# Decoder layer on one core: context loads behind the next x, expert weights split and a routed product moved ahead of the barrier

## The reference

```
x = x + attn(layernorm(x))          # own layernorm again, attention over the 256 features of a sequence, projection, + its input
x = x + xattn(layernorm(x), ctx)    # c, c2q, c*c2q, c*q2c concatenated, times W_l
x = x + moe(layernorm(x))           # 8 experts of 256 -> 128 -> 256, 4 chosen per token by grouped routing, and a shared one
```

## Time and profile before

| | us |
|---|---|
| median of 3 runs (lowest, highest) | 705.83 (705.38, 708.27) |
| profiled execution | 705.53 |
| its span | 703.7 |
| TensorE busy in it | 665.9 |
| mean granted clock of TensorE (1 is 2.4 GHz, 0.5 is 1.2 GHz) | 0.992 |
| VectorE, ScalarE, POOL busy | 474.3, 359.3, 249.8 |

### The profile page before, as it was taken

How to read it: one execution, slowest core, us unless ns; L and a number is a source line. 1 busy time by engine, 2 the same in 40 slices (tenths; PEclk the granted TensorE clock), 3 DMA queues, 4 the chain that set the end, 5 groups by cost and what they waited for, 6 DMA issues and landing times. The chain is left out here.

```text
span 703.7 us, 11790 instructions
## 1 busy us (share of the span) xinstructions
PE 665.9 (95%) x3880; PEld 563.4 (80%) x3880; DVE 474.3 (67%) x1237; ACT 359.3 (51%) x826; POOL 249.8 (35%) x321
## 2 busy tenths in 40 slices
PE   3999999899999999999989879999999999999997
PEld 2778878778788788787877767888888888888886
DVE  4488675676776776767778977666766666676433
ACT  3656674665667566756666536342333424234321
POOL 2136264064172462641734403232223222222231
PEclk9999999899999999999999999999999999999999
DMA  8616044043052150430541443321213232130300
GB/s 215 167 27 172 10 111 117 0 117 110 0 167 60 49 171 7 113 114 0 165 134 31 116 170 112 121 90 58 104 50 121 89 120 89 46 125 11 122 30 31
DMA packets 51775, 64.44 MB, mean 92 GB/s; under 512 B 3913, under 2 KB 49529, under 8 KB 50849
## 3 DMA queue, kind: packets, MB, share of 16 engines
q1 hardware_dynamic: 51744, 64.06, 30.0%
HBM read 56.60 MB, written 7.45 MB: 91 GB/s over the span
## 5 line engine op out<-in xcount | busy, mean ns | idle before, releaser
L1575 POOL TENSOR_TENSOR xt<-xt,cw_wide 128x512 f32<-128x512 f32 x56 | 74.3, 1326 | 192.7 <-ACT xt L1534 174.7
L1599 DVE TENSOR_TENSOR res<-bank,xt 128x512 f32<-128x512 f32 x62 | 42.6, 686 | 58.5 <-POOL xt L1575 54.1
L1538 ACT ACTIVATE a_hi<-res 128x512 fp32r<-128x512 f32 x42 | 26.6, 634 | 104.0 <-DVE res L1599 104.0
L75 PE MATMUL bank<-h_hi,w_lo 128*128 128x512 f32 x168 | 67.7, 403 | 1.6 <-DVE w_lo L1616 0.8
L76 PE MATMUL bank<-h_lo,w_hi 128*128 128x512 f32 x168 | 66.3, 395 | 0.0
L77 PE MATMUL bank<-h_hi,w_hi 128*128 128x512 f32 x168 | 66.3, 395 | 0.0
L75 PE MATMUL bank<-wp_hi,op_lo 128*128 128x256 f32 x128 | 40.8, 319 | 11.5 <-DVE op_lo L1111 11.0
L1001 POOL TENSOR_TENSOR wz_lo<-tmp,wz_hi 128x512 fp32r<-128x512 f32 x28 | 36.8, 1322 | 34.4 <-ACT wz_hi L769 34.1
L1604 DVE TENSOR_TENSOR a_lo<-res,a_hi 128x512 fp32r<-128x512 f32 x42 | 33.8, 804 | 22.4 <-ACT a_hi L1538 22.4
L624 PE MATMUL bank<-ctxf,qg 125*112 125x256 f32 x192 | 46.7, 379 | 0.0
L611 PE MATMUL bank<-cw_wide,ctw 128*112 128x375 f32 x128 | 46.3, 484 | 0.0
(11 more groups left out here) (250 smaller groups left out, 2138.8 us busy)
## 6 DMA issues: line engine op xcount, KB each, us to landing
cw_wide<-in_ctx_t SPq DMA_DIRECT2D x32, 375.0 KB
ctxf<-in_ctx SPq DMA_DIRECT2D x32, 375.0 KB
cw_wide<-cw_scratch SPq DMA_DIRECT2D x7, 1536.0 KB, 7.8
xt<-in_x SPq DMA_DIRECT2D x8, 448.0 KB, 10.4
x_scratch<-x2b SPq DMA_DIRECT2D x8, 448.0 KB, 3.3
x2n<-x_scratch SPq DMA_DIRECT2D x7, 512.0 KB, 4.7
cw_wide<-cw_scratch SPq DMA_DIRECT2D x7, 512.0 KB, 4.4
x2t<-x_scratch SPq DMA_DIRECT2D x7, 512.0 KB, 4.0
```

The costliest lines, as they stand in the source:

```text
L75: pe.matmul(dst, a_lo, b_hi, start=first, stop=False, **kw)
L1575: pool.tensor_tensor(sg[b][:, :], sg[b][:, :], cw_wide[p][:, ORDER[n], :], ALU.mult).then_inc(sgw_ok, 1)
L1599: dve.tensor_tensor(af[b][:, :], u_bank[b][:, :], sg[b][:, :], ALU.mult).then_inc(af_ok, 1)
```

## The change

- The queue of transfers: context 0 and 1 of the next group are issued as before. Context 2 and 3 are issued in the next pass, behind the next x. Behind the loop: the first x2n, then the shared expert, context 2 and 3 of the last group, experts 0 and 1, the second x2n.
- Last group, ScalarE: the shared expert's high split goes from behind the first h3 copies to ahead of the first exponential; expert 2's high split is new behind the loading of the silu table.
- Last group, POOL: expert 1's low split goes from ahead of c_lo to behind the x2b sums; expert 2's low split and the weighting of expert 0's silu follow it.
- Last group, TensorE: gate/up of expert 1 goes from behind the last c products to ahead of the second 512 tokens' transposes.
- Last group, VectorE: the product of expert 0 is new at the end.
- Second block, group 0: these steps fall away; the next group's logits, routing and cw transposes come one expert later.
- The split buffers of expert 2 are kept through both blocks; the projection's weights lie in them in the first.

```diff
+                def load_shared():
+                    sp.wait_ge(wl_lo_ok, 2)
...
                 def group(i, last):
...
                     if last:
+                        load_shared()
+                    if not is_first(i):
+                        for j in range(2, G):
+                            sp.wait_ge(c2q_mm, G * (i - 1) + j + 1)
+                            sp.wait_ge(w_in, 16)
+                            load_context(batch, j)
+                    if last:
+                        load_first_experts()
                         sp.wait_ge(h3_ok, T)
                         sp.wait_ge(x2_st, 16 * 4)
                         load_norm(sp, 1)
...
                     if not last:
-                        for j in range(G):
+                        for j in range(2):
                             sp.wait_ge(c2q_mm, G * i + j + 1)
                             sp.wait_ge(w_in, 16)
                             load_context(batch + G, j)
...
                         gate_up_early(1, wqkv_hi[:, 0, :], wqkv_lo[:, 0, :])
+                        pe.wait_ge(af_ok, 1)
+                        pe.wait_ge(w01_lo_ok, 2)
+                        gate_up_early(0, wqkv_hi[:, 1, :], wqkv_lo[:, 1, :])
                         pe.wait_ge(cwt_ok, 1)
                         pe.wait_ge(cb_ok, i + 1)
                         turn_h3(pe, 1)
                         for j in range(G):
                             z_c(i, j)
-                        pe.wait_ge(af_ok, 1)
-                        pe.wait_ge(w01_lo_ok, 2)
-                        gate_up_early(0, wqkv_hi[:, 1, :], wqkv_lo[:, 1, :])
...
+                    if last:
+                        act.wait_ge(shared_in, 48)
+                        act.activation(shared_hi[:, 0:GU + D], shared_f[:, :], ACT.Copy).then_inc(shared_hi_ok, 1)
                     exps(0)
...
                         act.activation(silu_warm[:, :], mhalf2[:, 0:1], ACT.Silu)
+                        act.wait_ge(wx_in[DONE], 48)
+                        act.activation(w2_hi[:, :], w_staged[0][:, :], ACT.Copy).then_inc(e_hi_ok, 1)
                         act.wait_ge(gu_mm, 1)
...
                         rstd3(pool, 1)
-                        w01_low(1)
                         pool.wait_ge(h3_ok, 2 * T)
...
                         pool.tensor_tensor(x2b[:, j, :], x1[:, j, :], bl_wide[:, :], ALU.add).then_inc(x1b_ok, 1)
+                    if last:
+                        w01_low(1)
+                        pool.wait_ge(e_hi_ok, 1)
+                        pool.tensor_tensor(w2_lo[:, :], w_staged[0][:, :], f32(w2_hi[:, :]), ALU.subtract).then_inc(e_lo_ok, 1)
+                        pool.wait_ge(sg_ok, 2)
+                        pool.wait_ge(cw_in, 16)
+                        pool.tensor_tensor(sg[1][:, :], sg[1][:, :], cw_wide0[:, 0, :], ALU.mult).then_inc(sgw_ok, 1)
...
                         x2_sum(i, 1)
+                        dve.wait_ge(gu_mm, 4)
+                        dve.wait_ge(sgw_ok, 1)
+                        dve.tensor_tensor(af[1][:, :], bank[3][:, :], sg[1][:, :], ALU.mult).then_inc(af_ok, 1)
...
                 def group(g, p, last):
+                    late = 1 if is_first(g) else 0
...
-                        if n == 2 and not last:
+                        if n == 2 + late and not last:
                             logits(pe, g + 1, h3_hi[1 - p], h3_lo[1 - p], h_bank[0])
```

More of the change, by code:

```diff
@@ L426, in _, with load_first_experts @@
                 sp.dma_start(wq[:, :], w_q).then_inc(early_in, 16)
+                def load_shared():
+                    sp.wait_ge(wl_lo_ok, 2)
+                    for half, w in enumerate((wg_s, wu_s)):
+                        sp.dma_start(gate_up_weights(shared_f)[:, half, :, :], w.rearrange("(k p) n -> p k n", p=P)).then_inc(shared_in, 16)
+                    sp.dma_start(shared_f[:, GU:GU + D], wd_s).then_inc(shared_in, 16)
+                def load_first_experts():
+                    for e in range(2):
+                        for half, w in enumerate((wg, wu)):
+                            sp.dma_start(gate_up_weights(w_f01[:, e, :])[:, half, :, :], w[e].rearrange("(k p) n -> p k n", p=P)).then_inc(w01_in, 16)
+                        sp.dma_start(w_f01[:, e, GU:GU + D], wd[e]).then_inc(w01_in, 16)
                 def group(i, last):
@@ L1499, in group @@
                         if not last:
-                            if n == 3:
+                            if n == 3 + late:
                                 pe.wait_ge(lgt_ok, g + 2)
@@ L1507, in group @@
                             turn_h3(pe, g + 1)
-                        if n == 6 and not last:
+                        if n == 6 + late and not last:
                             turn_cw(pe, g + 1, h_bank[0])
-                        if n == 2 and not last:
+                        if n == 2 + late and not last:
                             logits(pe, g + 1, h3_hi[1 - p], h3_lo[1 - p], h_bank[0])
-                        if n == 3 and not last:
+                        if n == 3 + late and not last:
                             turn_logits(pe, g + 1)
@@ L1548, in group @@
                                 h3_high(act, g + 1, h3_hi[1 - p])
-                            if n == 6:
+                            if n == 6 + late:
                                 copy_cw(act, g + 1, h_bank[0])
@@ L1579, in group @@
                         rstd3(pool, g + 1)
-                    for n in range(1, NE):
+                    for n in range(2 if is_first(g) else 1, NE):
                         expert(g, p, n)
@@ L1620, in group @@
                         moments3(dve, g + 1)
+                    late = 1 if is_first(g) else 0
                     for n in range(NE):
-                        if is_first(g) and n == 1:
-                            split_low(n + 2)
-                        if not is_first(g) or n >= 1:
+                        if not is_first(g) or n >= DONE:
                             product(g, p, n)
@@ L1636, in group @@
                             act_low(g, p, n)
-                        if n == 3 and not last:
+                        if n == 3 + late and not last:
                             sum_logits(dve, g + 1)
                             route_groups(dve, g + 1)
-                        if n == 4 and not last:
+                        if n == 4 + late and not last:
                             route_experts(dve, g + 1)
```

33 lines of the change are left out of this document (12 added, 21 removed).

## The result

The changed kernel takes 685.59 us (median of 4 runs, 685.23 to 687.39), where the kernel before took 705.61 beside it (704.49 to 708.27): ratio 0.9717, 95% interval 0.9691 to 0.9742, a gain of 20.0 us. The prediction was 689.5 with a range of 685.5 to 695.5: the gain was foreseen as 16.0, so it was 4 us too small.

What follows compares the result with a forecast made beforehand. TensorE was taken as the bound, working 665.9 of 703.7 us. Gains of 10.7 + 2.3 + 1.5 - 1.4 + 2.95 = 16.0 us, off the profiled 705.53, gave 689.5 us, range 685.5 to 695.5.

Steps and rivals of the forecast that it cites:

- Part 1: Loop loads: with context 2 and 3 behind the next x, VectorE's 5.76 us wait goes; gain 10.7 us.
- six times 46.09 is 276.54: Loop: six passes at 46.09 us busy time taken as the floor, against 287.27, so the loop loses 10.7.
- Parts 2 and 3: Last group: earlier x2n removes TensorE's wait, gain 2.3; moving POOL's split of expert 1 away gains 1.5 us.
- Part 4: Stretch up to the barrier: POOL's splits delay the routing and VectorE's tail the barrier; 1.4 us lost.
- its wait of 2.4: Ahead of the barrier: cw transposes wait 2.4 us for the delayed routing, with TensorE's whole queue behind them.
- Two splits of 1.81 therefore hold the routing for about 1.7 + 1.6 = 3.3 us: Ahead of the barrier: POOL's splits of experts 1 and 2 block VectorE's expert routing, ending at 408.75 instead of 405.45.
- Part 5: Behind the barrier: splits and product gone, logits an expert later, so the wait at the logits goes; gain 2.95 us.
- The term of 1.44 for half clock: Behind the barrier: half clock at logits and gate/up 3 goes with the 2.37 us wait; gain 1.44.
- the wait at gate/up 8: Behind the barrier: later routing on VectorE makes gate/up 8 wait 1.7 us where gate/up 7 waited 0.84.
- The clock rule: TensorE's last stretch: two new waits of 1.7 and 2.4 us may each bring half clock; the sum included none.
- pile-up: Rival near the barrier: both collisions in full plus one or two half-clock stretches; 692 to 695 us, chance 0.22.
- the blocking is slight: Rival: POOL's splits barely hold the routing; Part 4 gains 1.1, gate/up wait stays 0.84; 686.2 us, chance 0.19.

Runs made afterwards that it cites:

- e7: Kernel before, old load order, with VectorE's statistics of the next x moved behind the probabilities' low halves: 690.69 us, ratio 0.9792.
- e1: Kernel before with only the new order of loads: 687.66 us, ratio 0.9760.
- c1: Changed kernel with one more POOL wait: expert 1's low split starts only after the last group's four x3 low halves: 684.75 us, ratio 0.9694.
- e4: Changed kernel with expert 0's weighting (POOL) and product (VectorE) back behind the barrier: 685.46 us, ratio 0.9727.
- c5: c4 with expert 0's weighting and product back behind the barrier: 683.02 us, ratio 0.9670.
- second trace: Nothing changed: the changed kernel run and profiled again in a later set: 685.53 us, ratio 0.9703.
- e5: Changed kernel with the next group's first logits, routing and cw transposes back at their old place, one expert earlier: 685.54 us, ratio 0.9721.
- e2: Changed kernel with the old order of loads, everything else new: 703.68 us, ratio 0.9971.
- e3: Changed kernel with POOL's low split of expert 1 back in its old place ahead of c's low halves: 683.75 us, ratio 0.9697.
- c3: Changed kernel with expert 1's low split in POOL's idle gap ahead of the norms of the second 512 tokens: 683.01 us, ratio 0.9691.
- e6: Changed kernel with expert 1's gate/up back behind the last c products: 686.25 us, ratio 0.9717.
- c4: c3 with VectorE's low half of the shared expert's product moved ahead of the q2c reduce: 682.32 us, ratio 0.9674.

## Why the prediction was right, and where it was not

**Part 1, the loads in the loop: right mechanism, mis-sized term.** 10.7 us forecast, 15.2 measured. X lands after 4.0, VectorE never waits, no pass waits for a context. The step that failed is "six times 46.09 is 276.54": it took busy time as the least a pass can take. Here are TensorE's timelines of a pass with a small wait, the fourth: first before the change, then after.

```profile
223.00 0.28 PE L77 MATMUL bank<-wz_hi,c_hi 128*112 128x256 f32 x1
224.06 0.38 PE L75 MATMUL bank<-wp_hi,op_lo 128*128 128x256 f32 x1 [0.78 <-DVE op_lo L1111]
224.28 0.28 PE L76 MATMUL bank<-wp_lo,op_hi 128*128 128x256 f32 x1
...
225.46 0.28 PE L77 MATMUL bank<-wp_hi,op_hi 128*128 128x256 f32 x1
225.70 0.39 PE L75 MATMUL bank<-wp_hi,op_lo 128*128 128x256 f32 x1
225.92 0.28 PE L76 MATMUL bank<-wp_lo,op_hi 128*128 128x256 f32 x1
```

```profile
212.90 0.28 PE L77 MATMUL bank<-wz_hi,c_hi 128*112 128x256 f32 x1
213.02 0.28 PE L75 MATMUL bank<-w_hi,op_lo 128*128 128x256 f32 x1
213.14 0.28 PE L76 MATMUL bank<-w_lo,op_hi 128*128 128x256 f32 x1
```

At full rate these matmuls start 0.12 us apart and each is recorded as 0.28 long. A wait is therefore recorded 0.16 short: from 223.00 to 224.06 are 1.06 us, 0.94 more than 0.12, of which the row calls 0.78 idle. The first matmul behind a wait holds the second for 0.22 instead of 0.12. And the next two projections, whose low halves come from VectorE one by one, each start 0.24 and 0.22 apart, with no idle time recorded at all, since 0.24 is shorter than 0.28. Together 0.94 + 0.10 + 0.22 + 0.21 = 1.47 of the 1.51 by which this pass became shorter, where the profile's idle column had 0.78. So 0.75 us per pass, or 4.5 in six, stood in the "busy" column. E7 shows that it is VectorE's lateness and not the transfers, for it goes when VectorE's order alone is changed. All of that could have been read in the trace of before.

**Parts 2 and 3, the last group up to Z: right, with part 2 0.7 too small.** 2.3 + 1.5 forecast, 4.51 measured. The kernel before against e1 puts the first at 2.98 (the same hidden share), and e1 against the changed kernel puts the second at 1.53 (41.59 less 40.06), as worked out from the earlier trace rows.

**Part 4, up to the barrier: about the right sum, by luck.** Z to X as a whole lost 1.88 where 1.4 was forecast. From Z to the cw transposes there were 10.16 us; the forecast adds its wait of 2.4 and makes 12.56, and 12.94 were measured. From the transposes to the barrier's exit it makes 12.1 (its 14.5 less the 2.4), and 12.24 were measured. But the 2.4 did not come as forecast: there was no wait at the transposes at all. The failed step is "Two splits of 1.81 therefore hold the routing for about 1.7 + 1.6 = 3.3 us". One split met the routing, not two, and what TensorE lost, it lost earlier: 1.3 for an x3 low half that took 2.14 us instead of 0.78 while a split stood ready behind POOL's sums, and 1.5 of half clock behind that wait, neither of which the sum had. With expert 1's split held back (c1) both meet the routing, and the 2.4 us ahead of the transposes are there as 2.14. The wait at the barrier had the right size (1.7; measured 2.21 and 1.73) but the product's 0.7 is not a term of its own: without it the wait is still 1.63 (e4, c5), where the store behind the last x2 sum ends last. The 0.5 for POOL's weighting was 0.5 in the first trace and 1.1 in the second.

**Part 5, behind the barrier: right in sum, with two terms off that nearly cancel.** 2.95 forecast; 2.38 measured, 3.31 in the second trace, whose clock stayed full there. The term of 1.44 for half clock was too large. In e1, which has the kernel before's order there, the same wait stands at the logits and no half clock follows:

```profile
404.32 0.40 PE L204 MATMUL bank<-h_lo,gate 128*16 128x512 f32 x1 [2.37 <-DVE h_lo L199]
```

Its X to N is 33.27, only 0.42 shorter than 33.69: TensorE then waits for VectorE further on, 0.50 at the cw transposes and 1.08 at gate/up 7 instead of 0.84. The other term off is the wait at gate/up 8, 1.7 in the sum, 0.82 and 1.08 measured. At full clock on both sides (e1 against the changed kernel's second trace) the order behind the barrier is worth 2.89. E5 takes the credit from the later logits: the gain is that of the split and product taken off VectorE.

**The clock rule.** The sum had no new half clock, and of the rival "pile-up" the one or two stretches came true (two in the first trace, one in the second), its time of 692 to 695 did not. The trace after has a fall of the kind that the prediction weighed, at a place where it had expected neither wait nor fall: two waits of 1.25 and 1.19 us, 4.3 us apart, and 3.4 us at 0.51. The five traces with that pair and a Z to S of 10.16 to 10.19, against e2, which has the pair and no fall (8.70), put the wait at 1.3 and the half clock at 1.5; in the eight traces with only the first wait it never fell (7.37 to 7.40). By the rule of the Trainium skill (TensorE: Matmul & The Clock Gate, Part 1: The HAM clock gate), that the clock follows how busy TensorE has lately been, the trace agrees in kind. It does not tell which wait will be punished: at the barrier the clock fell behind waits of 2.21 (after) and 0.54 with 1.73 (e3), and not behind 2.03 (c3) or 0.53 with 1.73 (c1); at the logits behind 2.37 (before) and 2.34 (e7), and not behind 2.37 in e1. That stays open.

**The sum.** 4.5 us too little in part 1, 0.7 in part 2, 0.5 and 0.6 too much in parts 4 and 5, and 0.4 lost in the stretches ahead of the first pass and behind N: 16.0 + 4.5 + 0.7 - 0.5 - 0.6 - 0.4 = 19.7, against 19.8 of span. That the time still lies in the range (685.59, lower end 685.5) is luck: the sum was 3.8 us off, and inside parts 4 and 5 single terms were further off than their sums show. The rival "the blocking is slight" named a time near the measured one (686.2) for a reason that did not hold: the blocking was not slight. Of the prediction's own signs of being wrong two appeared, cw transposes without a wait and half clock near the barrier. Of its signs of being right, passes of 46.1 became 45.34; equal passes at clock 1.00, no wait of VectorE for x in the loop or for x2n, and no wait at the logits came as written.

## What to carry to other kernels

Price a wait of TensorE from start to start against the usual spacing of its matmuls, not by the idle column, and look at the followers too: a producer that is late for one tile is late by a little for the next ones, and none of that shows as idle. Before moving work to POOL, list what VectorE does beside it at its new place and at the instant the queue ahead of it empties, for that is when it starts; here a gap of 4.6 us earlier in the group took the same split for nothing and was worth 2.5 us by the medians. When a wait goes, look for it at the next barrier before counting it as gained (e6). And ask of a barrier what comes last on each engine, the queue of transfers too: an operation added on an engine that is not last costs only what it reaches beyond the others (0.1 us for the product).

## What the runs showed that was not expected

**POOL's queue decides how long VectorE is held.** VectorE's first x3 low half has two SBUF inputs and meets the four x2b sums of POOL. The instructions on the sums' tile in the changed kernel, then in c1 (durations in ns, least, median and most; first and last start):

```profile
L1060 POOL TENSOR_TENSOR x2b<-x,bl_wide x4: 719/796/878, 378.3 to 380.5; 112x256 f32<-112x256 f32 x4
```

```profile
L1060 POOL TENSOR_TENSOR x2b<-x,bl_wide x4: 872/905/1014, 378.1 to 380.8; 112x256 f32<-112x256 f32 x4
```

In the six traces in which expert 1's split stood ready behind the sums (after twice, e2, e4, e5, e6), the four sums took 3.07 to 3.09 us and the low half 2.14. In the eight without (before, e1, e3, e7, c1, c3, c4, c5), the sums took 3.58 to 3.61 and the low half 0.78. Not one trace falls between. The Trainium skill (SBUF — State Buffer, SBUF: two separate sides) says that a VectorE operation with two SBUF inputs (or in a mode that uses both ports) and a GpSimd operation that reads SBUF exclude each other for the whole instruction, and that the one that starts first has the ports. The first half agrees with the routing steps beside a split (1.95 for 0.42). The second says nothing of who is next; by the times here VectorE was let in behind the first of the sums, or passed over for more than one of them, depending on what stood at the end of POOL's queue. Why a later instruction should matter to the first sum is not settled by these runs.

**A small operation can be the one that pays.** In c3 and e3 expert 2's split met VectorE's reduce of 256 elements a partition (0.42, unharmed) and then a one-input operation on 32 elements, which took 1.28 and 1.29 instead of 0.18. So in a list of what a split on POOL may hold up, operations of one input belong too.
